# GAT attention on one core: ScalarE makes one tile's split exponent in every fourth pass

## What is computed

```python
h = (x @ W).reshape(n, HEADS, C)
a_s = jnp.einsum('nhc,hc->nh', h, att_src)
a_d = jnp.einsum('nhc,hc->nh', h, att_dst)
e = jax.nn.leaky_relu(a_s[src] + a_d[dst], NEG_SLOPE)
m = jax.ops.segment_max(e, dst, num_segments=n)
p = jnp.exp(e - m[dst])
z = jax.ops.segment_sum(p, dst, num_segments=n)
alpha = p / (z[dst] + EPS_SOFTMAX)
out = jax.ops.segment_sum(h[src] * alpha[:, :, None], dst, num_segments=n)
```

## Time and profile before

| | us |
|---|---|
| median of 3 runs | 2930.45 (2929.94 to 2932.85) |
| the profiled execution | 2929.37 |
| its span, first to last instruction | 2927.7 |
| busy in the span: PE / DVE / ACT | 2393.8 / 2007.1 / 1787.0 |
| `gat_rows`, from its first `span` (1137.9) to about 2085 | 947.1 |
| busy in these 947.1 us: PE / DVE / ACT / POOL | 790.87 / 884.00 / 654.40 / 42.40 |

### The profile page before, as it was taken

One profiled execution on the slowest core, in us unless ns is written; L12 is line 12 of the kernel. 1 busy time (PEld: TensorE's weight loads), 2 busy tenths in 40 slices (PEclk: granted clock), 3 DMA queues, 4 the chain that ended last, 5 costly groups with the idle time before them and its releaser, 6 DMA issues. The chain is left out here.

```text
span 2927.7 us, 62500 instructions
## 1 busy us (share of the span) xinstructions
PE 2393.8 (82%) x16906; PEld 1621.4 (55%) x16907; DVE 2007.1 (69%) x3577; ACT 1787.0 (61%) x4164; POOL 476.1 (16%) x825
## 2 busy tenths in 40 slices
PE   1988998988998954888888888888649999959795
PEld 1444444544544543666666666666527777735453
DVE  6777767777770026999999999998555555466175
ACT  1998989999990014766666667766338888610101
POOL 1444444444440000000000000000000000001010
PEclk7999999999999967999999999999869999979897
DMA  1222222222228605222222222222123333058193
GB/s 39 101 105 97 103 97 103 103 103 103 109 103 328 248 5 196 76 84 79 80 83 88 91 91 91 91 92 70 52 92 116 112 112 113 21 224 359 34 426 130
DMA packets 132818, 347.78 MB, mean 119 GB/s; under 512 B 14025, under 2 KB 115004, under 8 KB 115772
## 3 DMA queue, kind: packets, MB, share of 16 engines
q1 hardware_dynamic: 132544, 345.22, 31.7%
HBM read 218.96 MB, written 126.23 MB: 118 GB/s over the span
## 5 line engine op out<-in xcount | busy, mean ns | idle before, releaser
L434 PE MATMUL ps_build<-OH,KEY 128*128 128x400 bf16 x4108 | 737.0, 339 | 82.3 <-ACT KEY L391 44.0
L391 ACT ACTIVATE KEY<-KEY,cols 128x128 bf16<-128x128 bf16 x2054 | 622.0, 398 | 96.8 <-DVE KEY L362 95.7
L434 PEld LDWEIGHTS ps_build<-OH,KEY 128*128 128x128 bf16 x4108 | 399.9, 99 | 419.8 <-DVE OH L366 84.6
L1083 ACT ACTIVATE gr_e<-gr_ps,att_cols 128x256 f32<-128x256 f32 (+1 forms) x1300 | 502.0, 485 | 212.5 <-PE gr_ps L990 210.0
L362 DVE TENSOR_SCALAR KEY<-iota_key,key_base,cols 128x128 bf16<-128x128 int16 x1027 | 388.0, 410 | 220.4 <-PE ps_build L434 193.1
L990 PE MATMUL gr_ps<-ident,gr_r 128*128 128x128 f32 x2500 | 389.0, 296 | 100.2 <-DVE gr_r L1179 86.6
L409 POOL TENSOR_TENSOR KEY<-KEY,cols 128x256 bf16<-128x256 bf16 (+1 forms) x627 | 377.2, 602 | 496.8 <-DVE KEY L362 496.8
L990 PEld LDWEIGHTS gr_ps<-ident,gr_r 128*128 128x128 f32 x2500 | 291.4, 150 | 183.8 <-issue 136.9
L1019 PE MATMUL gr_ps<-gr_e,heads 128*33 128x128 f32 x5000 | 364.9, 277 | 25.5 <-DVE gr_e L1186 25.5
L1186 DVE SCALAR_TENSOR_TENSOR gr_e<-gr_e,gr_count_t 128x3072 f32<-128x3072 f32 (+1 forms) x104 | 349.5, 3361 | 36.1 <-ACT gr_count_t L1100 23.4
L1152 DVE CUSTOM_DVE_ANT_0 gr_unread<-gr_src_rows,gr_closed 128x3125 bf16<-128x3125 f32 (+1 forms) x100 | 344.4, 3444 | 19.6 <-DMA gr_src_rows<-gat_rows_d 15.2
(11 more groups left out here) (275 smaller groups left out, 1997.6 us busy)
## 6 DMA issues: line engine op xcount, KB each, us to landing
adjacency<-stage SPq DMA_DIRECT2D x200, 400.0 KB, 2.5
sage_ring<-count_by_source SPq DMA_DIRECT2D x50, 1600.0 KB, 8.8
agg_gcn_ring<-adjacency SPq DMA_DIRECT2D x25, 1600.0 KB, 8.4
gr_count<-adjacency SPq DMA_DIRECT2D x25, 1600.0 KB, 7.9
ar_counts<-adjacency SPq DMA_DIRECT2D x25, 1600.0 KB, 6.7
count_by_source<-gr_count_t SPq DMA_DIRECT2D x12, 3200.0 KB, 18.7
gr_src_rows<-gat_rows_d SPq DMA_DIRECT2D x4, 1600.0 KB, 19.5
fg_node<-gat_node_sums SPq DMA_DIRECT2D x1, 1650.0 KB, 6.3
```

What stands on the lines that cost most here:

```text
L391: last = act.activation(KEY[:, slot + j, v, :], KEY[:, slot + j, 0, :], ACT.Copy, scale=k.cols[:, 1 + v, bass.ds(c + j, 1)])
L434: last = pe.matmul(ps[:, 2 * (s % 2) + (v > 0), 0:SL], KEY[:, slot + j, v, :], OH[:, slot + j, :], start=slot == s % 2 * (BODY + 1) and j ...
L1083: last = act.activation(e[:, s, 0:w], ps[:, i % RINGS, c:c + w], ACT.Exp, bias=cols[:, h, s:s + 1])
```

## The change

In the fourth pass of a super-tile of two tiles (12 of the 13), DVE makes the split exponent of the first tile only. That of the second is made by ACT, since max(s + lift, floor) = relu(s + (lift - floor)) + floor. ACT does it in two instructions over 128x3125, a Relu with bias `over` and an Identity with bias `floor_u`, in place, with a wait on its own semaphore `lifted` between them. DVE makes the column `over` in `level`, once for each super-tile, with a wait on `levelled` before it. PE's first turned piece of that pass waits for `spanned` as well. ACT waits for `turned` of the third pass and for `over_ready` before it writes.

```diff
+        SHARED = HEADS - 1
+        over = sb("gr_over", [P, 1])
+        over_ready, lifted, spanned = map(sem, ("gr_over_ready", "gr_lifted", "gr_spanned"))
@@ turn_piece, PE
                 if i == 0:
                     pe.wait_ge(ranged, u + 1)
+                    if h == SHARED and width(g) == TWO:
+                        pe.wait_ge(spanned, g + 1)
@@ ACT
+            def span(g):
+                part = r[:, 1, 0:N]
+                act.wait_ge(turned, (g * HEADS + SHARED) * PIECES)
+                act.wait_ge(over_ready, g + 1)
+                act.activation(part, src_rows[:, SHARED, 0:N], ACT.Relu, bias=over[:]).then_inc(lifted, 1)
+                act.wait_ge(lifted, g + 1)
+                act.activation(part, part, ACT.Identity, bias=floor_u[:, SHARED, 1:2]).then_inc(spanned, 1)
@@ super_tile, ACT
+                    if h == SHARED and width(g) == TWO:
+                        span(g)
                     for i in range(PIECES):
                         power(g, h, i)
@@ level, DVE
+                if h == SHARED and w == TWO:
+                    dve.wait_ge(levelled, g * HEADS + (h + 1))
+                    dve.tensor_tensor(over[:], lift_u[:, h, 1:2], floor_u[:, h, 1:2], ALU.subtract).then_inc(over_ready, 1)
@@ span, DVE
-                for j in range(width(g)):
+                mine = 1 if h == SHARED else width(g)
+                for j in range(mine):
```

## The result

| | before | changed |
|---|---|---|
| median of 4 runs, us | 2930.56 (2929.94 to 2932.85) | 2951.34 (2950.73 to 2953.48) |
| profiled execution; its span | 2929.37; 2927.7 | 2950.85; 2949.2 |
| busy in the span: PE / DVE / ACT | 2393.8 / 2007.1 / 1787.0 | 2416.6 / 1993.2 / 1857.3 |

The ratio is 1.0071, 95% interval 1.0053 to 1.0088: **20.8 us slower**. The forecast was 17.5 slower. DVE has 13.9 us less work, ACT has 70.3 more, and PE 22.8 more, although PE's program did not grow by one matmul. PE's 22.8 us are the first thing to explain.

The account below looks back on a forecast made before the run. DVE was taken to set the pace. Seven super-tiles at +2.4 us and five at +0.5 summed to 19.3, taken as +17.5 on the 2930.45 median, so 2948; range 2926 to 2970.

Parts of the forecast that it names:

- DVE shorter by 1.82: In the fourth pass DVE makes one `span` instruction instead of two (3.64 us), saving 1.82 us a super-tile.
- `over` +0.2: One small DVE instruction with a wait in the second pass, without slack: +0.2 us a super-tile, bounds 0.16 and 0.3.
- ACT's passes: ACT's two passes before the fourth pass's burst: 2.905 us each, 5.92 with the wait between, bounds 5.7 and 6.2.
- When it starts: ACT's pair starts behind `keep`, so PE's fourth burst starts 2.3 us later after a slow third burst, 0.35 after a fast one.
- `weigh_first`: DVE's fourth-pass `weigh_first` waits for 12 exponentials: +0.9 to +1.9 us after a slow third burst, -1.1 to 0.0 after a fast one.
- PE's lateness: PE runs late into the next super-tile, lengthening DVE's stall for counts by 0.6 us (mixed clock) or 1.1 (low).
- the weights: Shares of slow bursts: fourth passes as 3 full, 3 mixed, 7 low of 13; third passes 7 slow, 5 fast.
- the both-slow case: A super-tile with a slow third burst and a low-clock fourth burst was priced at +3.2 us.
- A: Third and fourth bursts always at low clock, twelve times 3.2 us: +38 us, 2968; chance 0.20.
- B: Faster: shifted PE standing times no longer bring the low clock in third and fourth bursts, 10.8 us gained, 2920; chance 0.10.
- the whole 1.62: Full gain a super-tile (2911), said to be out of reach: ACT would have to end before DVE's old `span` does.
- C: No difference, about 2932: fourth burst at full clock and third as traced, or third nearly all fast and fourth mixed; chance 0.18.

Follow-up runs that it names:

- e4: Changed kernel without ACT's two passes and PE's wait for them, the second tile's fourth-pass split exponent left out: 2915.0 us, ratio 0.9950.
- e1: Kernel before with the column `over` alone, DVE making both tiles' split exponents: 2934.11 us, ratio 1.0009.
- e10: Changed kernel with ACT's passes ahead of `keep` and matmuls of zeros on PE before the third and fourth passes' bursts: 2913.51 us, ratio 0.9937.
- e11: Changed kernel with ACT making only 2300 of the second tile's 3125 columns, ahead of `keep`, DVE the others, no fillers: 2920.43 us, ratio 0.9962.
- e2: Changed kernel with twelve matmuls of zeros on PE before both the third and the fourth pass's burst: 2920.45 us, ratio 0.9962.
- e5: Changed kernel with the matmuls of zeros on PE before the third pass's burst alone: 2929.59 us, ratio 0.9996.
- e7: Changed kernel with ACT's two passes put ahead of `keep` of the third pass instead of behind it: 2930.73 us, ratio 0.9999.
- e6: Changed kernel with the matmuls of zeros on PE before the fourth pass's burst alone: 2931.0 us, ratio 0.9999.

## Why the prediction was right, point by point

The sign, the mechanism and nearly the size were right: 2948 was forecast, 2951.3 measured, in the range. By its steps:

1. DVE shorter by 1.82: right, e4 gave 1.64 a super-tile with `over` in it. DVE's busy time in the stage fell by 18.0, from 884.0 to 866.0, where some 21 was forecast; PE's rose by 22.1 there, which is the slow bursts.
2. `over` +0.2: right, by T to T in e1.
3. ACT's passes: 2.906 and 2.901 against 2.905 each. The pair took 5.85 (1575.09 to 1580.94) against 5.92, since the wait between the two cost 0.04, not 0.1. The Trainium skill, "ScalarE: Activation LUTs", section "What ACT_TABLE_LOAD costs", gave an estimate of 2.88 for one; the rows are 0.02 above it. The same page's "Rules for kernel authors" say of relu and add: "Use VectorE, not ScalarE". The rows agree as far as 5.8 us on ACT stand for 1.8 on DVE, but e10 and e11 show that the trade can pay.
4. When it starts: right. T to PE's burst is 24.53 (1581.07 - 1556.54), forecast 24.4 (1573.5 - 1549.09). The start lay 0.14 behind `keep`'s start and not behind its end, which makes up for the rest. PE stood 3.41, forecast 3.45.
5. `weigh_first`: +2.06 measured, +1.9 forecast with both bursts slow.
6. PE's lateness: overpriced. The stall grew by 0.58 and 0.32, not by 1.1 and 0.6. The step's lengths were good: from the burst's start to the end of `gather_first` are 19.57 us where 19.7 was estimated. But its own numbers give less lateness than it says: 1573.5 + 19.7 less 1579.75 + 12.1 is 1.35 and not 1.6, and the mixed case gives 0.9 and not 1.1. Measured it is 1.1 (the next burst at 1600.57, 13.2 behind `weigh_first` instead of 12.1) and 0.9, and with the 0.5 that goes into a wait, as forecast, that leaves the 0.6 and 0.3 of the stall.

What failed is **the weights**, at the end of step 6. I took the fourth pass as 10 slow of 13 and the third passes as traced, 7 of 12. They were 12 of 12 and 11 of 12, so the old places could not be carried over. That shifting one burst shifts the other is argued from the times, and was not tested alone. The price for the both-slow case was 3.2, measured 2.8. Of the eleven first, six had a fourth burst of about 4.5 and, but for the first of them, a third of 4.3, which cost 0.3; a third burst of 4.3 I had priced like one of 5.38 (+1.9 with a mixed fourth). So more slow bursts than forecast at a lower price, and a term that was missing, the twelfth super-tile (+3.9), which I had priced like the others. These errors partly cancel, and that 17.5 came so near 20.8 is in part luck: with the places as they turned out (one super-tile at 0.0, five at +3.2, six at +1.9) the prediction's own prices give +27.4.

The rivals. A, both bursts always slow, came true in its condition in eleven of twelve, but its price holds for 5.38 twice, and only five of twelve were that. B, faster, was right about its lever: with both bursts at full clock the same change takes 2920.45 (e2), and B said 2920. Its last sentence, that the whole 1.62 isn't to be had, holds for the place behind `keep`: e2 gives 1.09, and ACT's pair ends 22.2 us behind T there, where DVE's old `span` ended at 22.0. Ahead of `keep` and at full clock the pair ends at 21.4 (e10), and the whole of it comes. So its condition, that ACT ends before DVE's old `span` does, stood the test, and only "the mask pair's 5.83 says no" did not: the pair can start earlier. C was refuted by the ratio's interval.

Not settled: why bursts of 5.38 and of 4.3 to 4.5 alternate in the changed kernel, and what decides between full clock and slow. The length of the stand alone doesn't: 3.41 us came before bursts of 2.84 and of 5.38 in e5, and so did 3.44 before the change. The runs show only that filling PE's idle time removed every slow third and fourth burst.

## What to carry to other kernels

Work that is handed to an idle engine costs what its end makes others wait, not its duration: here the two passes stood behind `keep`, and moving them ahead of it was worth 20.6 us (2951.3 to 2930.7), part of it by milder slow bursts. Then look at what the waiting does to PE: after stands of 3.4 us every fourth burst of the changed kernel took 4.39 to 5.38 us instead of 2.84, and twelve matmuls of zeros in each of two idle places of PE gave 31 us back in the changed kernel and nothing in the one before, where DVE hid the slow bursts. Size the share so that the helper is done when PE wants the data (1600 columns: full clock in 11 of 12 fourth bursts), and price the last round of a loop apart, where other work around it is missing.

## What the runs showed that I had not expected

- A slow clock after a short stand: 2.62 us idle, then a burst of 4.31 us at a mean granted clock of 0.64, and slow bursts in 11 of 12 fourth passes of e7. The shortest such stand in the third and fourth passes of these runs was 2.05 us, before a burst of 4.07 in e11.
- Slow bursts settle into a pattern: T to T alternates 78.06 and 75.53 in the changed kernel and is 75.07 or 75.12 throughout in e7 and e6.
- ACT with a bias column on f32 from SBUF took 2.906 us for 3125 columns and 1.63 for 1600: 0.84 ns a column and 0.3 us besides. An ACTIVATE that waits for the one before it through its own semaphore starts 0.04 us after that one's end.
